# Four transformer blocks on one core: the turn of the score maxima issued behind the next maxima and scores, and its copy behind the next reduction

## The chip, the cores and the metric

One NeuronCore of a Trainium2 chip runs the whole kernel in one launch. The metric is device microseconds of that core; lower is better. Times given are single executions, and the median of three for the kernel before.

## The reference, cut to what matters

`x` is (32 sequences, 128 tokens, 144 channels); `cond_1152` is (32, 144). Four blocks follow each other, each with its own weights:

```
mod = silu(c) @ w_ada + b_ada               # shift, scale, gate, twice
h   = norm(x) * (1 + scale) + shift
q, k, v = split(h @ w_qkv + b_qkv)          # 16 heads of 9 channels
a   = softmax(q k^T / 3)                    # 128 x 128 for each head and sequence
x   = x + gate * ((a v) @ w_proj + b_proj)
h   = norm(x) * (1 + scale2) + shift2
x   = x + gate2 * mlp(h)                    # 144 -> 576 -> 144, gelu
```

Block 0's MLP is four experts, of which two are weighed per token. Block 2 uses RMS norms, also on q and k of each head. Block 3 has another attention layout in memory but the same arithmetic. The change touches only the softmax's maxima, in all four blocks.

## The kernel before, in words

Everything is written by hand: each engine has its own program, and semaphores with counted values join them. `X` stays in SBUF. Work is cut into groups of four sequences, `n = 0..31`, eight to a block ("layer"). The attention of a layer loops over `g` (group) and, in it, over eight units `u`; `U = 8n + u` counts units through all layers. A unit is one sequence and 8 of its 16 heads, so units `2P` and `2P+1` are the pair of one sequence.

For each unit the softmax goes in these steps, each by a small function:

- `scores_for_max(l, U)` (TensorE, L648): 8 matmuls of q by k with the query on the partitions, into PSUM banks 0 and 1. There is one such buffer, so it waits until `head_max(U-1)` has read it (`d_sm`).
- `head_max(l, U)` (VectorE, L1567): one reduction, 128 x 1024 f32 to 8 negated maxima, written to `negm`.
- `turn_max(P)` (TensorE, L655): one bf16 transpose of the pair's maxima from `negm` into bank 7. It waits for both units' `head_max` (`d_sm`) and for the copy before it (`d_mt`); in the loop a wait for `d_on` stands ahead of it, since bank 7 is also where `to_tokens` writes, and `normed` must have read that.
- `max_out(P)` (VectorE, L1574): the copy of the turned maxima from bank 7 to `mT`.
- `scores(l, U)` (TensorE, L666 and L670): 8 matmuls of k by q with the key on the partitions into banks 2 and 3, and 8 that add the negated maximum from `mT`. It waits for `d_mt` of its pair and for the exponential of two units earlier.
- `weights` (ScalarE, L1259): the exponential of a unit's scores, to `prob`.
- `weigh(U)` (TensorE, L682): probabilities by values, into bank 4. ScalarE copies a pair of them to `OT` (L1264).
- `to_tokens(nb)` (TensorE, L690): four transposes of `OT` into bank 7. It waits for `d_mt`, so that the turned maxima in bank 7 have been copied, and for `d_on`.
- `normed(nb)` (VectorE, L1583 reciprocal, L1585 product, which counts `d_on`): from bank 7 to `On`.

The maxima run ahead (`AHEAD = 5` units), the scores one unit ahead, the turns of a pair three units ahead. The order in which an engine does them is that of its program, written out by hand: no planner has a part in it. Before, unit `u` on TensorE was: in odd units the `d_on` wait and `turn_max((U+3)//2)`; then `scores_for_max(U+5)`; `scores(U+1)`; in even units `to_tokens`; in odd units `weigh` of both units of the pair; and between them the unit's share of the projections: `on_main`, `on_rem`, `project` (L713, L714) for the group before, `q_and_k` (L604, L605) and `values` (L636, L637) for the group two ahead. VectorE's order was: in odd units `max_out`; in some units `rest1` (L1528, what q and k have beyond their bf16 part); `head_max(U+5)`; in even units `normed`; then `mod_rem`, `split_rem`, `split_out` (L1591), `gated` (L1597) and `stats` (L1487, L1492) by unit.

The q and k of group n+2 leave TensorE in units 0 to 2 of group n (2 to 4 in layer 2), are split by ScalarE, VectorE (`rest1`) and GpSimd into bf16 parts, are written to DRAM by SyncE's queue and read back in another layout (L448), and `scores_for_max` needs them in unit 3 of group n+1.

The MLP of a layer follows its attention, with its first matmuls at L947/L948 or L959/L960 and its second at L976 or L996. It holds no edited line.

Of the kernel before, what the change touches and what calls it, by code (L numbers as in the profile page):

```python
# [49 lines left out]
AHEAD = 5  # L50
# [56 lines left out]
def build(nc, io):  # L107
    ctx = ExitStack()
    with ctx:
# [189 lines left out]

        def operand(l, side, n, U, s, i):  # L300

# [240 lines left out]
        def _(pe):  # L542
# [96 lines left out]

            def scores_for_max(l, U):  # L640
                n = U // UNITS
                pe.wait_ge(d_sm, CR + U)
                if U % UNITS == 0:
                    for s in range(2):
                        pe.wait_ge(q_r[n % 3][s], fetched(n))
                for i in range(4):
                    for s in range(2):
                        mm = pe.matmul(bank[s][:, T * i:T * i + T], operand(l, 0, n, U, s, i),  # L648
                                       operand(l, 1, n, U, s, i), start=True, stop=True)
                mm.then_inc(s_sm, 1)  # L650
# [101 lines left out]
            def attention(l):  # L752
                n0, m0, last = 8 * l, 16 * l, 64 * l + 64
                if l == 0:
                    layer_mods(0)
                    turn_mods(0)
                    t_rem(0, 5)
                    t_main(0, 6)
                    pe.wait_ge(q_w0, 16)
                    pe.wait_ge(d_ws, CR + 1)  # L760
                    pe.wait_ge(d_set, CR + 2)
                    for m in range(3):
                        q_and_k(l, 0, m, m)
                    layer_mods(1)
                    t_rem(1, 5)
                    t_main(1, 6)
                    pe.wait_ge(d_mod, CR + 1)
                    values(l, 0, 0, 3)
                    values(l, 0, 1, 4)
                    for m in range(3):  # L770
                        pe.wait_ge(d_r1, CR + m + 1)
                        q_and_k(l, 1, m, m)
                    pe.wait_ge(a_v, CR + 2)
                    turn_mods(1)
                    layer_mods(2)
                    pe.wait_ge(d_hm, CR + 8)
                    t_rem(2, 5)
                    pe.wait_ge(a_ht, CR + 8)
                    t_main(2, 6)
                    turn_mods(2)  # L780
                    layer_mods(3)
                    turn_mods(3)
                    pe.wait_ge(d_mod, CR + 4)
                    values(l, 1, 0, 3)
                    values(l, 1, 1, 4)
                    pe.wait_ge(d_r1, CR + 6)
                    pe.wait_ge(a_v, CR + 4)
                    pe.wait_ge(a_gt, CR + L)
                    pe.wait_ge(d_set, CR + 3)
                    start_layer(l)  # L790
                else:
                    if l == 2:
                        pe.wait_ge(a_qt, CR + 4 * 3)
                    turn_max(32 * l + 1)
                for g in range(8):
                    n, m = n0 + g, m0 + g
                    new = turned_at(l, g)
                    for u in range(UNITS):
                        U = UNITS * n + u
                        if u % 2 == 1 and U + 3 < last:  # L800
                            if U - 1 > 64 * l:
                                pe.wait_ge(d_on, CR + (U - 1) // 2)
                            turn_max((U + 3) // 2)
                        if U + AHEAD < last:
                            scores_for_max(l, U + AHEAD)
                        if U + 1 < last:
                            scores(l, U + 1)
                        if u % 2 == 0 and (g or u):
                            nb = U // 2 - 1
                            pe.wait_ge(d_mt, CR + min(nb + 3, last // 2))  # L810
                            pe.wait_ge(d_on, CR + nb)
                            to_tokens(nb)
                        if l == 0 and (g, u) == (6, 6):
                            pe.wait_ge(a_ht, CR + 4 * (NTH[m0 + 9] + 1))
                            gate_logits(0, 6)
                        if l == 0 and (g, u) == (7, 0):
                            turn_logits(0, 6)
                        if l == 0 and (g, u) == (7, 5):
                            turn_weights(0, 6)
                        if u == 1:  # L820
                            pe.wait_ge(a_v, CR + 2 * n + 2)
                            if g == 0 and l > 0:
                                pe.wait_ge(d_gate, CR + 2 * m0)
                        if u % 2 == 1:
                            weigh(U - 1)
                            weigh(U)
                        if u == 0 and new is not None:
                            if g == 0:
                                if l:
                                    pe.wait_ge(d_gate, CR + 2 * m0)  # L830
                            elif l == 3:
                                pe.wait_ge(a_vt, CR + 2 * (n + 1 - 24) + 2)
                            else:
                                pe.wait_ge(a_v, CR + 2 * (n + 1) + 2)
                            t_rem(new, 5)
                        if u == 1 and g > 0:
                            if new is not None:
                                pe.wait_ge(d_hm, CR + 4 * (NTH[new] + 1))
                            else:
                                pe.wait_ge(d_gate, CR + 2 * (m - 1))  # L840
                            on_main(n - 1, 5)
                        if u == 2 and g > 0:
                            pe.wait_ge(a_ont, CR + n)
                            on_rem(n - 1, 5)
                        if u == 3 and g > 0:
                            project(l, n - 1, 0, 5)
                        if u == 4 and g > 0:
                            pe.wait_ge(d_gate, CR + 2 * m - 1)
                            project(l, n - 1, 1, 5)
                        if l == 2:  # L850
                            by_token_unit(g, u, n, m, new)
                            continue
                        if u < 3 and g < 6:
                            if u:
                                pe.wait_ge(d_r1, CR + 3 * (n + 2) + u)
                            elif g and l == 3:
                                pe.wait_ge(a_vt, CR + 2 * (n + 1 - 24) + 1)
                            elif g:
                                pe.wait_ge(a_v, CR + 2 * (n + 1) + 1)
                            q_and_k(l, n + 2, u, 6)  # L860
                        if u == 3 and new is not None:
                            if g < 6:
                                pe.wait_ge(d_r1, CR + 3 * (n + 2) + 3)
                            elif l == 3:
                                pe.wait_ge(a_vt, CR + 2 * (n + 1 - 24) + 1)
                            else:
                                pe.wait_ge(a_v, CR + 2 * (n + 1) + 1)
                            t_main(new, 6)
                        if l == 3:
                            values_unit(g, u, n, m, new)  # L870
                        elif u == 6 and g < 6:
                            pe.wait_ge(a_ht, CR + 4 * (NTH[new] + 1))
                            values(l, n + 2, 0, 6)
                            if g:
                                pe.wait_ge(d_gate, CR + 2 * m)
                            else:
                                pe.wait_ge(d_hm, CR + 4 * (NTH[new] + 1))
                            values(l, n + 2, 1, 5)
# [576 lines left out]
        def _(dve):  # L1455
# [147 lines left out]
            def attention(l):  # L1603
                n0, m0, last = 8 * l, 16 * l, 64 * l + 64
# [44 lines left out]
                for g in range(8):  # L1649
# [3 lines left out]
                    q0 = 2 if l == 2 else 0  # L1653
                    for u in range(UNITS):
                        U = UNITS * n + u
                        if u % 2 == 1 and U + 3 < last:
                            max_out((U + 3) // 2)
                        if q0 < u <= q0 + 3 and g < 6:
                            rest1(n + 2, u - q0 - 1, 6)
                        if U + AHEAD < last:  # L1660
                            head_max(l, U + AHEAD)
                        if u % 2 == 0 and (g or u):
                            normed(U // 2 - 1)
                        if l == 2 and g < 6 and u == 0:
# [530 lines left out]
```

## Time and profile before

| | us |
|---|---|
| runs | 1526.88, 1531.16, 1750.05 |
| median of the runs | 1531.16 |
| profiled execution, its own time | 1525.55 |
| its span in the profile | 1523.7 |
| attention stages: layer 0, 1, 2, 3 | about 63 to 242, 571 to 752, 877 to 1091, 1200 to 1429 |

The attention stages are read off the first turn or maxima and the last weighing of a layer. How to read the rows: a line number (L655) names the instruction's line in the kernel. PE is TensorE's matmuls, PEld its weight loads, DVE VectorE, ACT ScalarE, SPq SyncE's queue. In the list of waits a row gives the engine and line, what it waited for, and then the total in us, the number of times and the longest. In a timeline a row gives the start and the length in us, the engine, line, operation, output and input, and in brackets the idle time before it and what ended it. PEclk is the granted TensorE clock, 1.00 being 2.4 GHz and 0.50 being 1.2 GHz.

### The profile page before, as it was taken

Reading aid. Unit: us, or ns where it says so; the run is one execution under the profiler, and the core shown is the slowest. Engines: PE = TensorE matmul, PEld = TensorE weight load, DVE = VectorE, ACT = ScalarE, POOL = GpSimd, SP = SyncE. Lnnn points to the kernel's source line nnn. Section 1 sums busy time; section 2 is a strip of 40 time slices with the busy share of each in tenths; the row PEclk is TensorE's granted clock in tenths of the full one; section 3 lists DMA queues with packets and bytes.
Section 4 is the critical chain, followed back from the end, with each engine's and each line's share of the span. In section 5 each row is a group of like instructions: output and inputs, shape, how many; then the busy total and the mean of one; then the engine's idle time right before and its main releaser. Section 6 shows DMA issues by size and latency. Waiting matters only on the chain. (4 is left out here: it accounts for less than half of the span.)

```text
span 1523.7 us, 41073 instructions
## 1 busy us (share of the span) xinstructions
PE 1402.7 (92%) x16016; PEld 1052.8 (69%) x16016; DVE 1025.8 (67%) x2537; ACT 780.9 (51%) x1290; POOL 568.9 (37%) x771
## 2 busy tenths in 40 slices
PE   5799988999999999998999878877999999999998
PEld 2477776777777776776777666665777677677776
DVE  4688885766776667888546698896446666566342
ACT  2376764333333336776644466665545465555543
POOL 3355542211131213554324544553325343343222
PEclk9699999999999999999999999999999999999999
DMA  4665641111122033454010443453116776784111
GB/s 129 156 151 150 160 104 53 52 45 44 36 63 80 15 93 89 133 146 135 18 32 17 111 112 100 103 127 95 34 36 86 126 110 119 129 133 92 30 50 48
DMA packets 209129, 134.94 MB, mean 89 GB/s; under 512 B 142461, under 2 KB 191320, under 8 KB 202730
## 3 DMA queue, kind: packets, MB, share of 16 engines
q1 hardware_dynamic: 188978, 129.74, 36.1%
q10 hardware_dynamic: 19960, 2.57, 1.2%
q8 instruction: 130, 2.13, 0.6%
q14 instruction: 61, 0.50, 0.1%
HBM read 98.24 MB, written 33.24 MB: 86 GB/s over the span
## 5 line engine op out<-in xcount | busy, mean ns | idle before, releaser
L1567 DVE TENSOR_REDUCE negm<-banks 128x8 bf16<-128x1024 f32 x256 | 311.1, 1215 | 82.4 <-PE banks L648 80.7
L1259 ACT ACTIVATE prob<-banks 128x1024 f32<-128x1024 f32 x256 | 262.3, 1025 | 179.5 <-PE banks L670 176.6
L2031 POOL TENSOR_TENSOR X<-X,gx 128x288 f32<-128x288 f32 x128 | 103.6, 822 | 267.8 <-DVE gx L1597 266.1
L1393 ACT ACTIVATE hid<-banks 128x512 f32<-128x512 f32 x144 | 85.9, 597 | 219.9 <-PE banks L960 219.9
L976 PEld LDWEIGHTS banks<-wfc,hid 128*128 128x128 f32 x1152 | 156.7, 190 | 32.3 <-issue 20.1
L666 PE MATMUL banks<-qk 54*128 54x128 bf16 (+1 forms) x2048 | 168.0, 235 | 3.5 <-ACT prob L1259 1.7
L670 PE MATMUL banks<-mT,identb 64*128 64x128 bf16 x2048 | 164.8, 224 | 0.0
L976 PE MATMUL banks<-wfc,hid 128*128 128x144 f32 x1152 | 161.6, 286 | 2.1 <-DVE hid L1767 2.1
L648 PE MATMUL banks<-qk 54*128 54x128 bf16 (+1 forms) x2048 | 122.1, 240 | 34.3 <-DVE negm L1567 13.2
L959 PE MATMUL banks<-hT,wfc 128*128 128x512 f32 x288 | 148.6, 597 | 1.0 <-DVE hid L1479 0.5
L682 PE MATMUL banks<-prob,V 128*32 128x128 f32 x4096 | 144.3, 283 | 1.8 <-issue 1.8
L1767 DVE TENSOR_TENSOR hid<-hid,qk 128x512 f32<-128x512 f32 x128 | 89.4, 700 | 75.0 <-ACT hid L1393 66.7
L1420 ACT ACTIVATE hid<-banks 128x512 f32<-128x512 f32 (+1 forms) x120 | 71.0, 596 | 121.7 <-PE banks L948 121.3
L1515 DVE TENSOR_SCALAR hmod<-banks,modr 64x128 f32<-64x128 f32 x256 | 86.8, 396 | 65.5 <-PE banks L581 65.2
L996 PE MATMUL banks<-wfc,hid 128*128 128x144 f32 (+1 forms) x960 | 130.1, 292 | 0.0
L996 PEld LDWEIGHTS banks<-wfc,hid 128*128 128x128 f32 (+1 forms) x960 | 125.4, 195 | 3.9 <-issue 2.7
L947 PE MATMUL banks<-hT,wfc 128*128 128x512 f32 x240 | 123.5, 595 | 0.0
L648 PEld LDWEIGHTS banks<-qk 54*128 54x128 bf16 (+1 forms) x2048 | 69.5, 101 | 76.6 <-issue 39.8
L682 PEld LDWEIGHTS banks<-prob,V 128*32 128x32 f32 x4096 | 107.2, 112 | 19.1 <-issue 8.4
L2002 POOL CAST parts<-res 96x512 bf16<-96x512 f32 x96 | 59.0, 615 | 161.2 <-DVE res L1528 160.3
L1199 ACT ACTIVATE hT<-banks,modm 128x128 f32<-128x128 f32 x256 | 98.8, 453 | 33.5 <-PE banks L574 33.5
L2004 POOL TENSOR_TENSOR parts<-res,parts 96x512 bf16<-96x512 f32 x96 | 112.0, 1166 | 7.8
(172 smaller groups left out, 2786.4 us busy)
## 6 DMA issues: line engine op xcount, KB each, us to landing
qk<-qk_scr SPq DMA_DIRECT2D x96, 216.0 KB
gbuf<-gate_scr SPq DMA_DIRECT2D x64, 288.0 KB, 4.5
qk_scr<-parts SPq DMA_DIRECT2D x48, 288.0 KB, 2.7
qk<-qk_scr SPq DMA_DIRECT2D x96, 144.0 KB
qk<-cw_scr SPq DMA_DIRECT2D x8, 1024.0 KB, 5.0
qk_scr<-parts SPq DMA_DIRECT2D x48, 144.0 KB, 2.4
qk<-qk_scr SPq DMA_DIRECT2D x96, 72.0 KB
qk<-tok_scr SPq DMA_DIRECT2D x32, 216.0 KB
```

The costliest lines, as they stand in the source:

```text
L648: mm = pe.matmul(bank[s][:, T * i:T * i + T], operand(l, 0, n, U, s, i), operand(l, 1, n, U, s, i), start=True, stop=True)
L666: pe.matmul(bank[2 + s][:, at], operand(l, 1, n, U, s, i), operand(l, 0, n, U, s, i), start=True, stop=False)
L670: mm = pe.matmul(bank[2 + s][:, at], one_hot(half, 64 * s + 4 * (u % 2) + i, [64, T]), mT[half, u // 2, :], start=False, stop=True)
L682: mm = pe.matmul(bank[4][32 * i:32 * i + 32, T * (2 * s + u % 2):T * (2 * s + u % 2 + 1)], V[:, n % 3, u // 2, VS * h:VS * h + 32], prob[: ...
L947: pe.matmul(bank[2 + i % 2][:], wfc1_t[:, at:at + 128], hT[:, h, :], start=True, stop=False)
L959: pe.matmul(bank[2 + i % 2][:], w, hT[:, h, :], start=True, stop=False)
L976: mm = pe.matmul(bank[4 + b // 2][:, C * (b % 2):C * (b % 2) + C], hid[:, i % KT, T * b:T * b + T], wfc2[:, e - (t == KT - 1), t, :], star ...
L996: mm = pe.matmul(bank[4 + q][:, C * (b % 2):C * (b % 2) + C], hid[0:rows, t, T * b:T * b + T], wfc2[0:rows, k, t, :], start=(t == 0), stop ...
L1259: act.activation(prob[:, 2 * (U % 3):2 * (U % 3) + 2, :], pairs[1][:], ACT.Exp, scale=scale).then_inc(a_exp, 1)
L1567: dve.tensor_reduce(negm[:, u // 2, :, 4 * (u % 2):4 * (u % 2) + 4], pairs[0][:].rearrange("q s (h k) -> q s h k", k=T), AX.X, ALU.max, ne ...
L2004: pool.tensor_tensor(parts[:, m, 2, :], res[:, i % 2, :], parts[:, m, 1, :], ALU.subtract).then_inc(g_p3, 1)
L2031: pool.tensor_tensor(x, x, gx[:, q, :, :], ALU.add).then_inc(g_x, 1)
```

## The change

On TensorE, in each odd unit, the `d_on` wait and `turn_max` move from ahead of `scores_for_max(U+5)` and `scores(U+1)` to behind both. On VectorE, in each odd unit, `max_out` moves from ahead of `rest1` and `head_max(U+5)` to behind both. No function changes inside.

```diff
@@ tensor, attention(l) @@
                     for u in range(UNITS):
                         U = UNITS * n + u
+                        if U + AHEAD < last:
+                            scores_for_max(l, U + AHEAD)
+                        if U + 1 < last:
+                            scores(l, U + 1)
                         if u % 2 == 1 and U + 3 < last:
                             if U - 1 > 64 * l:
                                 pe.wait_ge(d_on, CR + (U - 1) // 2)
                             turn_max((U + 3) // 2)
-                        if U + AHEAD < last:
-                            scores_for_max(l, U + AHEAD)
-                        if U + 1 < last:
-                            scores(l, U + 1)
                         if u % 2 == 0 and (g or u):
@@ vector, attention(l) @@
                     for u in range(UNITS):
                         U = UNITS * n + u
-                        if u % 2 == 1 and U + 3 < last:
-                            max_out((U + 3) // 2)
                         if q0 < u <= q0 + 3 and g < 6:
                             rest1(n + 2, u - q0 - 1, 6)
                         if U + AHEAD < last:
                             head_max(l, U + AHEAD)
+                        if u % 2 == 1 and U + 3 < last:
+                            max_out((U + 3) // 2)
                         if u % 2 == 0 and (g or u):
                             normed(U // 2 - 1)
```

## Rows read from the trace of the kernel before

**Rows 1.** The page, part 1: busy us (share of the span) and instructions.

```profile
PE 1402.7 (92%) x16016; PEld 1052.8 (69%) x16016; DVE 1025.8 (67%) x2537; ACT 780.9 (51%) x1290; POOL 568.9 (37%) x771
```

**Rows 2.** Windows: busy times in the attention stages of layers 0, 2 and 3.

```profile
core 0: us, PE busy (x) PEld busy (x) DVE busy (x) ACT busy (x) POOL busy (x), PEclk, DMA share, GB/s
63.00:242.00 179.00, 164.92 (x3019) 125.61 (x3015) 150.42 (x337) 122.19 (x175) 87.63 (x109) 0.97 0.54 134
877.00:1091.00 214.00, 172.62 (x3067) 139.90 (x3064) 174.61 (x391) 133.84 (x218) 105.47 (x160) 0.95 0.38 98
1200.00:1429.00 229.00, 217.22 (x3125) 164.58 (x3123) 145.22 (x297) 129.96 (x190) 85.68 (x113) 0.97 0.63 111
```

**Rows 3.** Waits: the whole span, then TensorE in layers 0, 1 and 3.

```profile
PEld banks L655 <- DVE On L1585: 59.6, 85, 1.7
...
PE banks L655 <- DVE On L1585: 28.3, 40, 1.4
...
DVE mT L1574 <- PE banks L655: 15.1, 27, 1.6
...
PE banks L655 <- DVE On L1585: 3.6, 6, 1.2
...
PE banks L655 <- DVE On L1585: 4.0, 8, 1.0
...
PE banks L655 <- DVE On L1585: 3.4, 6, 0.8
```

**Rows 4.** Timeline: layer 0, group 2, units 3 to 6; then a unit 7.

```profile
120.57 1.21 DVE L1567 TENSOR_REDUCE negm<-banks 128x8 bf16<-128x1024 f32 x1
...
121.41 0.79 PE L605 MATMUL banks<-hr,rqkv 66*96 66x512 f32 x1
...
121.98 0.31 DVE L1585 TENSOR_TENSOR On<-banks,rec 128x144 f32<-128x144 f32 x1
...
122.34 0.10 PEld L655 LDWEIGHTS banks<-identb,negm 128*128 128x128 bf16 x1 [0.79 <-DVE On L1585]
...
122.51 0.40 PE L648 MATMUL banks<-qk 54*128 54x128 bf16 x8
...
123.30 1.08 PE L682 MATMUL banks<-prob,V 128*32 128x128 f32 x32
...
128.80 0.20 DVE L1574 COPY mT<-banks 128x128 bf16<-128x128 bf16 x1
...
128.92 1.22 DVE L1567 TENSOR_REDUCE negm<-banks 128x8 bf16<-128x1024 f32 x1
...
130.20 0.40 PE L648 MATMUL banks<-qk 54*128 54x128 bf16 x8 [0.30 <-DVE negm L1567]
...
201.23 0.32 PE L637 MATMUL banks<-rqkv,hr 66*128 66x144 f32 x1
...
201.40 0.23 PE L655 MATMUL banks<-identb,negm 128*128 128x128 bf16 x1
```

**Rows 5.** The chain that ended last, layer 2: first and last of five reads.

```profile
935.71 10.37 DMA qk<-qk_scr
...
1049.88 11.47 DMA qk<-qk_scr
```

**Rows 6.** Waits of TensorE: 877 to 925, 925 to 1061.5, 1061.5 to 1091, layer 3.

```profile
PE banks L655 <- DVE On L1585: 4.1, 4, 1.4
...
PE banks L655 <- DVE On L1585: 11.4, 13, 1.3
PE banks L648 <- DMA qk<-qk_scr: 8.8, 5, 3.9
...
PE banks L655 <- DVE On L1585: 1.9, 3, 0.8
...
PE banks L648 <- DMA qk<-tok_scr: 7.0, 4, 3.1
```

**Rows 7.** Windows: layer 2, ahead of and behind a read's landing (columns: rows 2).

```profile
942.00:946.20 4.20, 1.92 (x21) 1.44 (x16) 4.07 (x7) 2.09 (x3) 0.57 (x2) 1.00 0.50 131
946.20:950.20 4.00, 3.99 (x62) 3.32 (x62) 1.23 (x1) 1.62 (x2) 1.73 (x2) 0.57 0.27 78
```

## The prediction

> **What bounds the kernel now.** I read the page first. TensorE is busy for 92% of the span [rows 1], so it is near the bound, but 8% of 1523.7 us is 121 us in which it stood. Then the same count for the attention stages [rows 2], since only they hold the edited loops: TensorE is busy 164.9 of 179 us in layer 0, 172.6 of 214 in layer 2, 217.2 of 229 in layer 3 (layer 1 is like layer 0). VectorE is close behind in layers 0 and 2 (150.4 and 174.6 us) and far behind in layer 3 (145.2). So a shorter stand of TensorE is worth its length only where neither VectorE nor a transfer sits right behind it.
>
> Then the waits of `turn_max` (L655) [rows 3]. It stands for `On` (L1585): 28.3 us by the matmul rows, 59.6 us by the weight loads. The first undercounts (the tail of earlier matmuls counts as busy), the second overcounts (the loads run ahead of the matmuls, and stand even where those don't). The truth is between, and a stretch of the timeline gives it per place [rows 4]. There `head_max` ends at 120.57 + 1.21 = 121.78, `normed`'s product ends at 121.98 + 0.31 = 122.29, and the turn starts at 122.34, 0.56 us behind `head_max`. `scores_for_max` (L648), which stands behind it in TensorE's queue, waited for nothing but the turn: it needs `head_max` only. A `scores_for_max` that does wait for `head_max` starts 0.06 us after it (130.20, with `head_max` ending at 128.92 + 1.22 = 130.14). So the order of before holds the next maxima back by at most 0.56 - 0.06 = 0.50 us for each odd unit, for a semaphore that they don't need.
>
> **The change, part by part.** No instruction is added or taken away; 120 turns and 120 copies move, 30 in each layer (the two at each layer's start stand outside the loops). Nothing that issues a DMA moves, and no DMA queue is passed by anything.
>
> (1) *TensorE: the turn goes behind `scores_for_max(U+5)` and `scores(U+1)`.* The turn keeps its own time: it is 0.23 us long, the next matmul starts 0.17 us after it, but most of that overlaps. What goes is the stand. Unit 3 of a middle group: the matmul before ends at 121.41 + 0.79 = 122.20 and the turn starts at 122.34, a gap of 0.14; where it doesn't wait it starts 0.15 us *before* the end of the one ahead (201.40 against 201.23 + 0.32 = 201.55) [rows 4]. So 0.14 + 0.15 = about 0.3 us are lost there, and all of it comes back, as `head_max` was done 0.42 us before 122.20. Unit 7 has no wait (the 201.40 row is one). Unit 1 has none in the middle groups either.
>
> Unit 5 loses about 0.26 us in the same way, but there VectorE is the bound: `scores_for_max` of unit 6 waits for `head_max` of unit 5 at 130.20, and this one began as soon as the copy let it. What comes back is only what the copy took ahead of it: copy at 128.80, `head_max` at 128.92, so 0.12 us.
>
> (2) *The wait for `d_on` moves with the turn.* Behind it in the queue now stand `weigh` and all the rest of the unit instead of the scores. It is covered: `On` is there 0.51 us after `head_max`, and between them TensorE now has `scores_for_max` and `scores`, which take 123.30 - 122.51 = 0.79 us by the rows until `weigh` starts. If that cover were gone the price would be the old one, 0.5 us per unit.
>
> (3) *VectorE: the copy goes behind `head_max(U+5)`.* It costs 0.2 us on VectorE either way. Its reader is `to_tokens` of the next unit, which stands behind another `scores_for_max`; that one itself waits for the same `head_max`, after which the copy is the next instruction. So the copy (0.2 us) has the whole of 0.4 us of maxima and 0.8 us of scores as cover. Could VectorE stand at the copy, for a turn that comes late? The turn is issued about 0.7 us after the maxima start and done by 1.0 us; `head_max` starts some 0.4 us after the maxima start (122.51 + 0.40, and its own latency) and ends 1.2 us later, at 1.6. Margin 0.6 us. Today VectorE stands 15.1 us at the copy, 27 times [rows 3]; I expect most of it to go, but it is mostly slack. Bounds for it: 0 and 5 us gained.
>
> **The sum.** Middle groups (about five in a layer): 0.30 + 0.12 = 0.42 us each in layers 0 and 1. At the layer's ends other work is missing and the stand is long; these are the waits that the matmul rows show: 3.6 us in 6, 4.0 us in 8, 3.4 us in 6 for layers 0, 1 and 3 [rows 3]. Each can give back 0.50 at most, the rest then goes to `head_max`.
> - Layer 0: 5 x 0.42 + 6 x 0.50 = 5.1. Layer 1: 5 x 0.42 + 8 x 0.45 (mean wait 4.0 / 8 is 0.5, and some have `head_max` in them) = 5.7.
> - Layer 3: TensorE is 95% busy and unit 3 doesn't wait in the middle groups; unit 5 by some 0.15 us. 6 x 0.50 + 4 x 0.15 = 3.6.
> - Layer 2 looks richest, and gives least. The chain of waits there goes through the reads of q and k, 10.4 to 11.5 us long, five groups in a row from 935.71 to 1049.88 [rows 5]. A group ends when its read lands, whatever TensorE did meanwhile. Of 17.4 us of stands for `On`, 11.4 lie in that stretch [rows 6] and will be turned into a longer wait for the DMA (now 8.8 us). Inside the stretch the chain from one landing to the next write passes unit 3's maxima, unit 4, and `rest1` of unit 5. It gets the turn after the landing instead of before it (+0.1 us) and loses the copy ahead of `rest1` (-0.12): nothing. Ahead of the stretch four waits of 4.1 us, of which the part before the first bound read counts, about 1.0; behind it three of 1.9 us give 3 x 0.50. Layer 2: 2.5.
> Together 16.9 us. From this I take 1 us for reads in layers 0, 1 and 3 that land with little to spare (layer 3 already waits 7.0 us for them, 4 times [rows 6]): 16 us.
>
> The profiled execution took 1525.55 us, span 1523.7 with 1.85 us around it; 1525.55 - 16 = 1509.5. The runs shown lie higher, two at 1526.9 and 1531.2 (the median), 3.5 us above the profiled one in the mean, so I expect about **1512 us**.
>
> **A rule that speaks against it.** In layer 2 TensorE is busy for 1.92 of 4.20 us before a landing, at a granted clock of 1.00, and in the 4.00 us behind it the clock is 0.57, a mix of the two levels with 1.2 GHz most of it [rows 7]. The change moves stands from before the turn into this wait. The Trainium skill, "TensorE: Matmul & The Clock Gate", section "HAM oscillation — how this bites in real kernels", says that a wait for DMA ahead of every tile can throttle the clock afresh each time; by it more of the landings would be followed by a slow stretch. The trace agrees for this landing.
>
> **Rivals.**
> - *The clock in layer 2.* One slow stretch: the 4.00 us at 0.57 do what 2.3 us do at full clock, a loss of 1.7 us. Total stand before a landing hardly changes, as both places are close together, but if three landings more fell slow, it is +5 us: 1514.5 + 2.5 = 1517. It counts inside the range.
> - *Hidden anyway.* VectorE or the reads take nearly all back in layers 0 and 1, as at unit 5. For it: VectorE is 84% busy in layer 0, and the unit 5 row. Against: at unit 3 `head_max` was done long before TensorE was free, so nothing else holds the maxima. Then only layer 3 and the ends give, 0.3 us at each of some 20 places: 6 us, so 1519.5 + 2.5 = 1522.
> - *The weight loads tell the truth.* 85 stands, less 27 in layer 2's stretch, 0.50 each: 29 us, so 1496.5 + 2.5 = 1499. Against it: a gap of 0.14 us is all the matmul rows show where the loads show 0.79.
> - *Slower: VectorE stands at the copy.* In units 1, 3 and 5 of layers 0 and 1 VectorE has no idle time, and behind the copy stand the products and statistics on which the next `head_max` waits. If the turn lands after `head_max` ends, each such copy holds them. It decides when the turn, now behind 16 score matmuls, is more than 1.6 us behind the start of the maxima; they took 0.79. With 1 us of delay (0.4 us of stand) at 3 units x 8 groups x 2 layers: +19 us, against some 5 us still gained: 1539.5 + 2.5 = 1542. Only a slow clock there would do it, and the clock is 0.97 in these stages [rows 2].
> - *It doesn't do what it says*: the turn would still hold the maxima. The code leaves no way for it; `scores_for_max` waits for `d_sm` alone.
>
> **Chances.** Forecast (10 to 22 us less): 0.64. Hidden or the clock (up to 10 less, or no change): 0.22. More than 22 less: 0.08. Slower than before: 0.06, and half of it under 2%. A measurement tells about 2%, 31 us. So faster by over 2%: 0.05; within 2%: 0.92; slower: 0.03. Range 1497 to 1527: its low end is the weight-load rival, its high end no change; beyond them lie about 0.1 of the chance.
>
> **What would show it right.** In the profile after: no wait of L655 for `On` worth a microsecond in any stage (28.3 us before); L648 in odd units starts 0.06 us after `head_max` or at once; L648's waits for `negm` up by a few us; L648's wait for the read in layer 2 up from 8.8 to about 15 us; hardly a wait of `mT` (L1574); TensorE's attention stages shorter by 5 to 6 us in layers 0 and 1, 2 to 3 in layer 2, 3 to 4 in layer 3, the MLP stages unchanged. It would be wrong if the waits vanish and the stages keep their length, if VectorE shows waits for L655 above the 15.1 us of now, or if layer 2 shortens by more than 5 us.

## The result, and the profile after

The changed kernel takes 1520.14 us (median of 18 runs, 1511.68 to 1542.13) where the kernel before takes 1528.39 us (18 runs beside it). The ratio is 0.9942, 95% interval 0.9924 to 0.996: 8.9 us less, with 6.1 to 11.6 us inside the interval. It lies within 2%, and within the range; the forecast was 16 us less, so the gain came out at little more than half. One slow run of each kernel (1750.05 and 1542.13 us) stands outside the ratio. The profiled execution has a span of 1512.9 us, 10.8 less than before.

The waits of the changed kernel, over the whole span, answer to [rows 3]:

```profile
DVE negm L1567 <- PE banks L648: 89.5, 80, 3.9
...
PEld banks L648 <- DVE negm L1567: 52.2, 82, 2.4
...
PE banks L648 <- DVE negm L1567: 23.0, 39, 2.2
...
PE banks L648 <- DMA qk<-qk_scr: 20.1, 10, 5.2
...
PE banks L581 <- POOL xr L1997: 12.4, 16, 1.8
```

The stand of the turn for `On` (28.3 us, 40 times) is gone from the list, and the copy's stand for the turn fell from 15.1 to 1.8 us. Both edits did what they say. But other stands of TensorE grew: for `head_max` from 13.2 to 23.0 us, for the reads of q and k from 9.2 to 20.1 us, for GpSimd's `xr` (L1997) from 9.2 to 12.4 us. Against the 28.3 us that went, these three grew by 23.9.

Busy times by attention stage answer to [rows 2]; the stages are those of layers 0, 1, 2 and 3:

```profile
core 0: us, PE busy (x) PEld busy (x) DVE busy (x) ACT busy (x) POOL busy (x), PEclk, DMA share, GB/s
63.00:241.00 178.00, 164.86 (x3013) 125.07 (x3007) 149.71 (x337) 122.80 (x176) 89.34 (x111) 0.98 0.55 136
569.00:746.00 177.00, 168.55 (x3045) 128.75 (x3046) 145.67 (x306) 124.47 (x179) 86.25 (x113) 1.00 0.42 112
866.00:1079.00 213.00, 171.34 (x3084) 138.24 (x3079) 175.74 (x393) 135.39 (x222) 106.13 (x161) 0.97 0.38 99
1188.00:1417.00 229.00, 221.36 (x3101) 164.98 (x3103) 142.77 (x295) 129.21 (x188) 84.52 (x112) 0.94 0.62 110
```

Layer 3 is the surprise: TensorE is busy 221.4 us where it was 217.2, for the same matmuls, at a granted clock of 0.94 where it was 0.97. One execution doesn't tell whether that belongs to the kernel, so both kernels were profiled twice more. Lengths in us, from a layer's first `head_max` (L1567) to the start of its last pair's weighing (L682), and between these:

| | before, three profiles | after, three profiles | difference of means | forecast |
|---|---|---|---|---|
| attention 0 | 185.5, 186.9, 188.1 | 184.1, 186.1, 185.5 | -1.6 | -5.1 |
| MLP 0 | 322.3, 322.0, 322.5 | 322.3, 322.4, 322.2 | 0.0 | 0 |
| attention 1 | 187.3, 185.8, 187.0 | 182.4, 181.8, 183.5 | -4.1 | -5.7 |
| MLP 1 | 118.8, 117.5, 117.5 | 115.0, 115.0, 117.5 | -2.1 | 0 |
| attention 2 | 220.2, 221.8, 221.9 | 218.2, 220.6, 220.6 | -1.5 | -2.5 |
| MLP 2 | 103.8, 103.7, 103.7 | 103.7, 103.7, 103.8 | 0.0 | 0 |
| attention 3 | 233.6, 234.2, 234.2 | 235.5, 231.7, 231.5 | -1.1 | -3.6 |
| span | 1523.7, 1524.7, 1526.5 | 1512.9, 1513.8, 1516.2 | -10.7 | -16 |

The attention stages gave 8.3 us, half of the 16.9 counted for them, and 2 us came from a stage that holds no edited line.

### The profile page after: what moved, and what is told of

Its sections match the earlier page's. It is cut to its first block and busy times, and to the rows that moved or that the text cites. A ratio compares the mean times of both kernels' runs of the same rounds, so it can differ in the third digit from the quotient of the medians.

```text
span 1512.9 us, 41073 instructions
## 1 busy us (share of the span) xinstructions
PE 1400.6 (93%) x16016; PEld 1047.5 (69%) x16016; DVE 1022.3 (68%) x2537; ACT 780.3 (52%) x1290; POOL 570.0 (38%) x771
## 5 line engine op out<-in xcount | busy, mean ns | idle before, releaser
L1567 DVE TENSOR_REDUCE negm<-banks 128x8 bf16<-128x1024 f32 x256 | 310.8, 1214 | 90.4 <-PE banks L648 89.5
L976 PEld LDWEIGHTS banks<-wfc,hid 128*128 128x128 f32 x1152 | 156.7, 190 | 32.3 <-issue 20.1
L648 PE MATMUL banks<-qk 54*128 54x128 bf16 (+1 forms) x2048 | 122.2, 240 | 53.8 <-DVE negm L1567 23.0
L648 PEld LDWEIGHTS banks<-qk 54*128 54x128 bf16 (+1 forms) x2048 | 69.6, 101 | 128.4 <-issue 68.5
L682 PE MATMUL banks<-prob,V 128*32 128x128 f32 x4096 | 141.3, 279 | 0.6 <-issue 0.6
L960 PE MATMUL banks<-hr,rfc 66*128 66x512 f32 x144 | 114.7, 797 | 0.0
```

Source lines behind the costliest of these rows:

```text
L682: mm = pe.matmul(bank[4][32 * i:32 * i + 32, T * (2 * s + u % 2):T * (2 * s + u % 2 + 1)], V[:, n % 3, u // 2, VS * h:VS * h + 32], prob[: ...
L960: pe.matmul(bank[2 + i % 2][:], x, hr[:, h, :], start=False, stop=True).then_inc(s_fc1, 1)
L976: mm = pe.matmul(bank[4 + b // 2][:, C * (b % 2):C * (b % 2) + C], hid[:, i % KT, T * b:T * b + T], wfc2[:, e - (t == KT - 1), t, :], star ...
L1567: dve.tensor_reduce(negm[:, u // 2, :, 4 * (u % 2):4 * (u % 2) + 4], pairs[0][:].rearrange("q s (h k) -> q s h k", k=T), AX.X, ALU.max, ne ...
```

## The experiments

### Each half alone

Theory: the gain needs `head_max(U+5)` to be freed of the turn, so it needs TensorE's half and VectorE's half. Rivals: one half has it all; or VectorE's stand at the copy is dear.

```diff
# pe_half: TensorE as after, VectorE as before
-  d_on wait, turn_max; scores_for_max(U+5); scores(U+1)
+  scores_for_max(U+5); scores(U+1); d_on wait, turn_max
# dve_half: VectorE as after, TensorE as before
-  max_out; rest1; head_max(U+5)
+  rest1; head_max(U+5); max_out
```

> Only TensorE's half: the turn stands behind the maxima and scores, VectorE's copy stays ahead of head_max. If VectorE standing at the copy is a real danger (the slower rival), head_max(U+5) now starts about 0.5 to 0.6 us later in each odd unit, which VectorE can't hide in units 1, 3, 5 of layers 0 to 2: +10 to +25 us against before, and VectorE's waits at mT rise from 15 us to over 60. If VectorE had room, the whole gain of the change is there with this half alone: -9 us.

> Only VectorE's half: the copy goes behind head_max, the turn stays ahead of the maxima on TensorE. If the gain comes from TensorE's stand at the turn, this is within 3 us of before, since head_max(U+5) still waits for maxima that stand behind the turn. If the gain is VectorE's order alone (0.12 us at unit 5, 0.2 us at others), it is -5 to -9 us, most of the change's.

Measured: pe_half 1530.6 us, ratio 1.0017 (0.999 to 1.0044). dve_half 1527.5 us, ratio 1.0003 (0.9983 to 1.0022). Neither half moves the time clear of noise; together they give 0.9942. In both halves the next maxima's reduction still waits for the turn, once through TensorE's queue, once through VectorE's. The waits of pe_half:

```profile
DVE mT L1574 <- PE banks L655: 89.0, 81, 5.3
```

VectorE stands 89 us at the copy, as foreseen (15.1 before), and yet the kernel is 2.6 us slower at most likely, not 10 to 25. The stand is not one that was added, though: VectorE's wait for the maxima (L648) fell from 80.7 to 48.8 us at the same time, and its idle time as a whole, the span less its busy time, is 497.8 us where it was 497.9. So the stand took the place of another. It isn't quite free either: middle groups of layer 1 (TensorE's L581 to the next) take 22.83 us, 0.41 more than before. And pe_half isn't the slower rival, which has the copy behind `head_max`; behind_weigh, below, is nearer to it.

### Where the middle groups' 0.42 us went: the turn's place

Theory A: behind the bf16 scores the turn costs TensorE more than it did ahead of the maxima, where it stands behind a float32 matmul. The timelines of before and after, layer 0, group 2, unit 3, show it. The kernel after:

```profile
120.15 0.79 PE L605 MATMUL banks<-hr,rqkv 66*96 66x512 f32 x1
...
120.88 0.40 PE L648 MATMUL banks<-qk 54*128 54x128 bf16 x8
...
121.67 0.23 PE L655 MATMUL banks<-identb,negm 128*128 128x128 bf16 x1
...
121.83 1.08 PE L682 MATMUL banks<-prob,V 128*32 128x128 f32 x32
```

From the float32 matmul's start to the maxima it is now 0.73 us, before it was 122.51 - 121.41 = 1.10 [rows 4]: 0.37 less. From the maxima to the weighing it is 0.95 us, before it was 123.30 - 122.51 = 0.79: 0.16 more. In unit 7, where before had no stand, the same two differences are 0.07 and 0.16 (0.33 to 0.26 us from L637 to L648, 0.79 to 0.95 us from L648 to L682). The step from 0.79 to 0.95 or 0.96 us stands in nearly every pair of layers 0 to 2, and layer 3 has it from 1.27 to 1.44 us. So the turn took 0.07 us where it stood and takes 0.16 us where it stands now, 0.09 us more in every odd unit. To test it, the turn was moved behind both `weigh`, which are float32:

```diff
# behind_weigh (and the same file again as weigh_again)
                         if U + 1 < last:
                             scores(l, U + 1)
-                        if u % 2 == 1 and U + 3 < last:
-                            ... turn_max((U + 3) // 2)
...
                         if u % 2 == 1:
                             weigh(U - 1)
                             weigh(U)
+                        if u % 2 == 1 and U + 3 < last:
+                            ... turn_max((U + 3) // 2)
# late_copy: besides, VectorE's max_out behind split_rem, gated and stats of the unit
```

> Turn behind both weighs, copy behind head_max. Theory A (place): behind bf16 scores the turn costs TensorE 0.16 us, behind a float32 matmul 0.07 us, because its start overlaps that one's tail; here it stands behind float32 weighs, so TensorE's issue is shorter by 0.09 us in 120 units, 11 us in all, and it is up to 8 us faster than the changed kernel unless VectorE now stands at the copy (turn lands about 2.0 us after the maxima start, head_max ends at 1.6: 0.4 us of stand in each odd unit, mT waits up to 40 us). Rival (hidden anyway): TensorE's order no longer matters, same time as the changed kernel within 2 us.

> As the one with the turn behind both weighs, but the copy stands behind split_rem, gated and stats of the odd unit, so that VectorE doesn't stand at it. Theory A (place): the 11 us of issue show without the stand: 5 to 10 us faster than the changed kernel, 1500 to 1506 in a profile. Rival (other bounds: GpSimd's xr in layer 0, the reads in layers 2 and 3): no more than 2 us faster than the changed kernel.

> Turn behind both weighs. Undisturbed groups of layer 0 were 0.30 us shorter than in the changed kernel (22.13 against 22.43). If that carries to the total in layers 0 and 1 and at part in layer 3, it is 2 to 6 us faster than the changed kernel, ratio 0.990 to 0.993. If reads and slow stretches of the clock take it back, the two are the same within 2 us.

The timeline of behind_weigh at the same place:

```profile
122.07 1.08 PE L682 MATMUL banks<-prob,V 128*32 128x128 f32 x32
...
123.08 0.23 PE L655 MATMUL banks<-identb,negm 128*128 128x128 bf16 x1
...
123.15 0.46 PE L713 MATMUL banks<-wproj,OnT 128*128 128x144 f32 x2
```

The projection's matmul starts 1.08 us behind the weighing's start; in the kernel after, with nothing between them, it was 1.01 (122.84 against 121.83). The turn costs 0.07 us there, and the maxima are back at 0.79 us ahead of the weighing. Per undisturbed group of layer 0 that is 0.29 us less than in the kernel after (table below). The mechanism of theory A is shown. But in the totals it isn't clear of noise: behind_weigh 1519.0 us, ratio 0.9931 (0.9905 to 0.9957); weigh_again 1518.5 us, 0.9943 (0.9918 to 0.9967); after_third, beside it, 1518.2 us, 0.9946 (0.9921 to 0.997); late_copy 1520.0 us, 0.9948 (0.9924 to 0.9973). None can be told from the changed kernel, so there is no version to prefer. Two things take the saving back: middle groups of layer 1 aren't shorter (22.38 us against 22.32 in the kernel after, next section), and TensorE's clock was lower (section on the clock).

behind_weigh also makes the slower rival, a turn that lands after `head_max` is done: VectorE stands at the copy (L1574) for the turn 27.5 us in 51 places, and the time is the changed kernel's. The rival had 0.4 us in 48 places at 19 us.

### Where the rest of it went: GpSimd sets half of an undisturbed group

A group of layers 0 and 1 can be cut at two marks on TensorE: `t_rem` (L581) in unit 0, which waits for GpSimd's `xr`, and the maxima (L648) at the head of unit 4. Rival: `xr` swallows what TensorE gains. To test it GpSimd's normalisation was cut short, in both orders: it leaves out 128 of 144 channels, so the output is wrong.

```diff
# short_before, short_after
             def rows(k):
...
-                    x = X[:, G * g + b, :]
+                    x = X[:, G * g + b, CM:C]
...
-                        pool.tensor_scalar(xn[:, p, b, :], x, ...
+                        pool.tensor_scalar(xn[:, p, b, CM:C], x, ...
```

> The order of before; GpSimd's rows normalise only the last 16 of 144 channels (the other 128 are left out), so that xr is ready some 2 us sooner. If GpSimd's xr sets the groups of layer 0, TensorE's wait of 1.0 us for it in unit 0 goes and a middle group falls from 22.55 by 0.5 to 1.0 us; if not, by less than 0.2.

> The order of after with the same short rows. If xr swallowed the change's gain in layer 0, a middle group is now 0.4 us shorter than in short_before; if the gain was given back by the turn's place (0.09 us in each of four odd units), it is 0.0 to 0.1 us shorter.

And TensorE's own work was cut, in the order of after, to see what a microsecond of it is worth. This kernel leaves out three of four turned outputs in units 0, 2 and 6:

```diff
# thin_after
-                            to_tokens(nb)
+                            to_tokens(nb, 4 if u == 4 or g == 0 else 1)
```

> The changed kernel with one transpose of four in to_tokens of units 0, 2 and 6 from the second group on (three quarters of these units' turned outputs are left out), which takes some 0.35 us of TensorE's time from each of the three units, about 1 us a group, without moving any order. If reads of q and k set the groups of layer 2, its groups 2 to 5 keep their mean within 0.3 us, while middle groups of layer 1 fall by 0.6 to 1 us; if TensorE set them, they fall by the same in both layers.

TensorE's marks in layer 0, group 5, none of them with a slow clock. The kernel before, after, and short_after:

```profile
182.57 0.60 PE L581 MATMUL banks<-ident,xr 128*64 128x128 f32 x4 [0.25 <-POOL xr L1997]
...
194.14 0.40 PE L648 MATMUL banks<-qk 54*128 54x128 bf16 x8
...
205.12 0.60 PE L581 MATMUL banks<-ident,xr 128*64 128x128 f32 x4 [0.25 <-POOL xr L1997]
```

```profile
181.19 0.60 PE L581 MATMUL banks<-ident,xr 128*64 128x128 f32 x4 [0.29 <-POOL xr L1997]
...
192.64 0.40 PE L648 MATMUL banks<-qk 54*128 54x128 bf16 x8
...
203.62 0.60 PE L581 MATMUL banks<-ident,xr 128*64 128x128 f32 x4 [0.29 <-POOL xr L1997]
```

```profile
181.52 0.60 PE L581 MATMUL banks<-ident,xr 128*64 128x128 f32 x4
...
192.97 0.40 PE L648 MATMUL banks<-qk 54*128 54x128 bf16 x8
...
203.48 0.60 PE L581 MATMUL banks<-ident,xr 128*64 128x128 f32 x4
```

Both parts of this group, by such rows of five kernels, and of group 4 for late_copy, in us:

| | unit 0 to unit 4 | unit 4 to the next unit 0 | group |
|---|---|---|---|
| before | 11.57 | 10.98 | 22.55 |
| after | 11.45 | 10.98 | 22.43 |
| behind_weigh | 11.16 | 10.98 | 22.14 |
| thin_after | 11.28 | 10.98 | 22.26 |
| short_after | 11.45 | 10.51 | 21.96 |
| late_copy (group 4) | 11.16 | 10.75 | 21.91 |

In this group the second part is the same to 0.01 us whatever TensorE has to do, until the work of VectorE or GpSimd is changed; when GpSimd's is cut, the bracket at L581 is gone. It is a chain: maxima of unit 4, `head_max`, `normed`, `gated`, `stats` of unit 4, `head_max` of unit 5, `stats` of unit 5 on VectorE; then `factor`, `rows` and `copies` on GpSimd; then `t_rem`. The copy stands in it before and after the change (ahead of unit 5's `head_max`, then ahead of its `stats`), so it lost nothing. late_copy, which has the copy behind these `stats`, shows it: its second part is 0.23 us shorter.

```profile
162.35 0.60 PE L581 MATMUL banks<-ident,xr 128*64 128x128 f32 x4
...
173.51 0.40 PE L648 MATMUL banks<-qk 54*128 54x128 bf16 x8
...
184.26 0.60 PE L581 MATMUL banks<-ident,xr 128*64 128x128 f32 x4
```

Nothing that TensorE saves in units 5 to 7 counts here: it stands longer at L581, no more. With the chain cut short in both orders (22.13 us for the group in short_before, 21.96 in short_after) the change is worth 0.17 us: that is between the two values that I had set, so `xr` hid a little of the gain, and the turn's place took more. The whole kernels took 1522.6 and 1525.1 us, one run each, which tells nothing between them. But short_after's layers aren't shorter for their shorter groups: its attention stages of layers 0 and 1 are 185.6 and 185.0 us long, the mean of the three profiles of after is 185.2 and 182.6. Two groups of layer 0 take 23.3 and 23.6 us there, with a stand of 1.5 us for a read of q and k. So the chain through GpSimd sets the groups that nothing else disturbs; that the layers would shrink without it isn't shown.

Layer 1 has the same marks but not the same constancy. The second part of its middle groups is 10.86 us before and after, 11.22 in behind_weigh and 11.31 in thin_after, while the first part is 11.56, 11.45, 11.16 and 11.29. GpSimd's part itself got longer there, in each of three groups: from its first normalisation (L1988) to the end of `xr` (L1997) it takes 4.02 us in the kernel after, 4.37 in behind_weigh and 4.47 in thin_after. The kernel after, then thin_after:

```profile
661.64 3.54 POOL L1988 TENSOR_SCALAR xn<-X,mv,rstd 128x144 f32<-128x144 f32 x4
665.25 0.41 POOL L1997 COPY xr<-xn 128x256 f32<-128x256 f32 x1
```

```profile
658.99 4.00 POOL L1988 TENSOR_SCALAR xn<-X,mv,rstd 128x144 f32<-128x144 f32 x4
663.06 0.40 POOL L1997 COPY xr<-xn 128x256 f32<-128x256 f32 x1
```

The same instructions run beside other ones of VectorE then; whether that is the cause no run shows.

thin_after asks the same of the whole kernel. It takes 28.6 us out of the time in which these transposes keep TensorE busy. (TensorE as a whole is busy for 17.3 us less, 1383.3 against 1400.6: the clock was lower in that profile, 0.972 against 0.977, so the rest took longer.) The kernel after, then thin_after, groups of instructions by line:

```profile
L690 PE MATMUL banks<-ident,OT 128*128 128x128 f32 x512 | 85.1, 290 | 0.5 <-ACT OT L1264 0.2
```

```profile
L690 PE MATMUL banks<-ident,OT 128*128 128x128 f32 x260 | 56.5, 301 | 0.5 <-ACT OT L1264 0.2
```

and its time is 1519.9 us, ratio 0.9955 (0.9931 to 0.9979), the changed kernel's own. Part of it came back as a longer wait for `xr`, 22.9 us where it was 12.4, and part of it, by an estimate, through the clock (section on the clock). The waits of thin_after:

```profile
PE banks L581 <- POOL xr L1997: 22.9, 19, 2.1
PE banks L648 <- DMA qk<-qk_scr: 21.9, 10, 4.4
```

As a test between the layers it failed. Groups 2 to 5 of layer 2 took 28.7 us in the mean, against 28.4, 28.6 and 28.8 in the three profiles of after (by the starts of their last pairs' weighings), which is what the reads' theory asks. But middle groups of layer 1 didn't fall by 0.6 to 1 us either, they rose from 22.32 to 22.60 us with GpSimd's part, so layer 2's constancy alone doesn't prove the reads. The reads are shown by the chain of after, layer 2, where six of them stand in a row, one more than in [rows 5]; the first, the second and the last:

```profile
897.21 10.89 DMA qk<-qk_scr
...
925.60 10.59 DMA qk<-qk_scr
...
1039.02 11.24 DMA qk<-qk_scr
```

### The clock

Theory: layer 3's 235.5 us and the 2 to 4 us of MLP 1 come from stretches in which TensorE's clock fell, and differ between executions of one kernel. Both files were run again for their profiles:

> The kernel before once more, for a second profile. If the lengths of layer 3 and the number of slow stretches of TensorE's clock belong to the kernel, its attention of layer 3 is again within 1 us of 233.6 us with about 20 us at half clock in it; if they are chance of one execution, it differs by 2 us or more.

> The changed kernel once more: ratio 0.994 within 0.002. The profile tells which differences hold: by the theory of place (turn behind scores costs 0.09 us more) middle groups of layers 0 and 1 take 22.4 to 22.6 us again, 0.1 us less than before; by the theory of a slow clock in layer 3, its 235.5 us and some 30 us at half clock change from execution to execution by 2 us or more.

> The changed kernel, beside the version with the turn behind the weighs: ratio 0.994 to 0.996. The attention of layer 0 in 184 to 186 us, of layer 1 in 182 us, the stage between layer 1's attention and layer 2's in 115.0 us if TensorE's clock doesn't fall in it, and 1.25 us more for each slow stretch of 3.4 us.

> The kernel before, third profile. Middle groups of layer 0 in 22.5 us again. If the slow stretches in the stage between the attentions of layers 1 and 2 come with the order of before, there are two or three again and it takes 117.5 to 119 us; if they are chance, there may be none and it takes 115.0.

The times: after_again 1519.9 us, ratio 0.9955 (0.9925 to 0.9985); before_again 1526.6 and before_third 1528.4 us, one run each. MLP 1 in the windows of before and after:

```profile
750.50:869.30 118.80, 109.16 (x630) 84.17 (x629) 62.54 (x195) 56.79 (x118) 47.96 (x76) 0.96 0.16 44
```

```profile
744.00:859.00 115.00, 105.10 (x626) 80.30 (x617) 62.59 (x195) 56.37 (x118) 48.07 (x75) 1.00 0.16 46
```

The same work, 3.8 us apart, at 0.96 and 1.00 of the clock. By the trace's clock records the half-rate time in this stage was 10.2 us in before, 6.8 in before_again and before_third; 0 in after and after_again, 6.8 in after_third; 3.4 in dve_half, which took 115.9 us. All fourteen profiles lie near one line: 115.0 us at full clock and about 1.2 us for each 3.4 us at half, up to 119.3 us. Layer 3's attention, the kernel after and after_again:

```profile
1181.00:1417.00 236.00, 228.36 (x3150) 171.03 (x3154) 147.59 (x303) 132.98 (x196) 84.52 (x112) 0.94 0.62 109
```

```profile
1185.00:1417.00 232.00, 223.41 (x3129) 168.19 (x3123) 147.54 (x301) 133.37 (x198) 83.82 (x110) 0.96 0.64 111
```

One kernel, 4 us apart. So the loss in layer 3 was this one execution's, and the length of MLP 1 is set by the clock, not by the edited order. Whether the order makes the clock fall there less often (3 of 3 profiles of before, 1 of 3 of after, but also 2 of 3 with the turn behind the weighs) is open. The same holds for attention 1, where each profile of before has 3.4 us at half rate and those of after 0, 0 and 3.4: by the line above that is some 0.8 of its 4.1 us.

Over whole executions more can be said, as each run has its granted clock. Means over the runs that the ratios rest on, with the us at half rate worked out as 2 x (1 - clock) x span:

| | runs | granted clock | us at half rate |
|---|---|---|---|
| before | 67 | 0.973 | 83 |
| after, with after_again and after_third | 34 | 0.973 | 82 |
| pe_half | 10 | 0.971 | 89 |
| dve_half | 10 | 0.972 | 85 |
| behind_weigh, weigh_again, late_copy | 29 | 0.970 | 90 |
| thin_after | 10 | 0.967 | 101 |

Before and after have the same clock, so the 8.9 us as a whole aren't the clock's. Most of the other versions have a lower one. At 1.2 us for 3.4 at half rate, the 8 us more of the turn behind the weighs cost about 3 us, and the 19 us more of thin_after about 7. These are estimates from the slope in MLP 1, and the means are good to 3 us or so at half rate; but they are of the size of what was missed: by them the turn behind the weighs would be about 3 us faster than the kernel after at an equal clock. What makes the clock fall more often in these versions isn't shown.

## Why the prediction was right or wrong

- **What bounds it.** "A shorter stand of TensorE is worth its length only where neither VectorE nor a transfer sits right behind it": right, and GpSimd was left out of it. In layer 0 TensorE waited for `xr` at L581 in the same timeline that I read for unit 3; in the list of waits it is 9.2 us in 12, below the rows that I counted.
- **Part (1), the stand.** Its size was right: unit 3 gained 0.37 us up to the maxima, of which 0.30 is the stand. That `scores_for_max` waits for `head_max` alone is right: the two halves show that it must be freed on both engines.
- **The step that failed is the term "middle groups: 0.30 + 0.12 = 0.42 us each"**, which measured 0.12 in layer 0 (22.55 to 22.43). "The turn keeps its own time" was wrong: it costs 0.16 us behind bf16 scores and 0.07 behind a float32 matmul. Two odd units in the part that TensorE sets take 0.18 of the 0.30. And the 0.12 of unit 5 wasn't there: the copy went from ahead of `head_max` to ahead of `stats`, and both are in the chain to `xr`. late_copy, with the copy behind these `stats`, is the version that gains there (0.23 us). With about 5 groups in each of two layers that is 3 us too much, of the 8.6 between the 16.9 counted and the 8.3 measured.
- **Layer 3.** 3.6 us were forecast; 1.1 came, where the three profiles of after alone lie 4 us apart. Its middle groups have no stand in unit 3 and all pay for the turn's place: the maxima of units 1, 3, 5 and 7 are followed by the next 0.16 us later, and units 0, 2, 4 and 6 give about 0.07 back. The same step is wrong here: at 0.09 us in four odd units, five middle groups lose 1.8 us (an estimate) where 0.6 was to be gained.
- **The ends.** They gave most of what there is: layer 1's groups 0, 5, 6 and 7, of 20.91, 22.97, 21.23 and 15.5 us before, became 20.27, 22.47, 20.66 and 14.8, 2.4 us together in the first two profiles. Layer 1's 4.1 us less five groups of 0.12 is 3.5, as counted (8 x 0.45). Layer 0's 1.6 us leaves 1.0 for its ends, where 3.0 were counted; why isn't shown, and its profiles lie 2 to 3 us apart.
- **Layer 2.** "Gives least": 1.5 us for 2.5 forecast. The stands inside the stretch of reads turned into a longer wait for them, 8.8 to 16.6 us in this layer (15 forecast; 16.1 and 14.7 in the other two profiles).
- **The rivals.** "Hidden anyway" had the right kind of cause, a chain behind TensorE, and a gain of 6 us; the result, 8.9, lies between it and the forecast. The chain that was found ends in GpSimd, which it didn't name, and it expected next to nothing of layer 1's groups, which gave 4.1 us with their ends. The weight-load rival (29 us) is out. The slower one had a mechanism that can be made: behind_weigh has 27.5 us of such stands, for a price of 19 us, and is no slower than the kernel after. The clock in layer 2 didn't fall more for the longer waits: at half rate it was 20.5, 27.3 and 20.5 us in the three profiles of before, 17.1, 30.7 and 23.9 in those of after. So the clock rule was put in the wrong place: the Trainium skill, "TensorE: Matmul & The Clock Gate", section "HAM oscillation — how this bites in real kernels", ties the fall to waits for DMA; the trace has such falls in layers 2 and 3, but the profiles' largest steady difference by the clock is in MLP 1.

## What to carry to other kernels

When a wait is taken off an engine's queue, look for the next chain that closes once per loop, on every engine, and cut the loop at its marks: a part that stays equal to 0.01 us when one engine's work is changed is set by something else, here by VectorE and GpSimd. Then change that too: in layer 1 the part that had been equal grew by 0.4 us as soon as the rest moved. When less work doesn't mean less time, compare the granted clocks before you blame a chain: here both had a share, the clock's by an estimate. A semaphore that holds back a producer through two in-order queues is only gone when it is gone from both. A moved instruction has no price of its own: measure it in its new neighbourhood, here 0.07 us behind float32 and 0.16 behind bf16.

## What the runs showed of the hardware

The same 128 x 128 bf16 transpose costs TensorE 0.16 us between bf16 matmuls and the weighing, and 0.07 us behind a float32 one, before whose end it starts (201.40 against 201.55 us in [rows 4]). Taking 28.6 us of matmul time from an engine that the page calls 93% busy changed nothing that can be measured in the time; its mean granted clock was 0.967 and not 0.973, which by the estimate above hides about 7 us. The same five GpSimd instructions took 4.02 us in the kernel after and 4.47 in thin_after, beside other instructions of VectorE. And three executions of one kernel differ by 2.5 to 4 us in one stage, by how much of it TensorE's clock spent at half rate.
